# Head outputs of an attention layer turned by VectorE in 32x32 squares, a gap in the V products around it, and four more heads' maxima beside the experts

## What is computed

```python
xn = _layernorm(x)
# attention, per batch and head (64 in all)
a1 = softmax(q1 @ k1.T * scale) @ v          # v: 1024 x 16
a2 = softmax(q2 @ k2.T * scale) @ v
o = a1 - lam * a2
o = _rms_norm(o, sub_norm_w) * (1 - LAMBDA_INIT)
attn = o.reshape(B, N, 256) @ w_proj.T + b_proj
# experts: each token goes to two of 8; 512 rows an expert and slot range
h = gelu(disp @ w_gate)                      # 1024 wide
eo = h @ w_down
out = x + attn + g1 * eo[f1] + g2 * eo[f2]
```

## Time and profile before

| | us |
|---|---|
| median of 3 runs (1751.41 to 1754.59) | 1751.65 |
| the profiled execution | 1751.97 |
| its span, first to last instruction | 1750.1 |

### The profile page before, as it was taken

How to read it: one execution, slowest core, us unless ns; L and a number is a source line. 1 busy time by engine, 2 the same in 40 slices (tenths; PEclk the granted TensorE clock), 3 DMA queues, 4 the chain that set the end, 5 groups by cost and what they waited for, 6 DMA issues and landing times.

```text
span 1750.1 us, 78852 instructions
## 1 busy us (share of the span) xinstructions
PE 1660.8 (95%) x34242; PEld 917.0 (52%) x34243; DVE 1477.7 (84%) x2482; ACT 1349.4 (77%) x2637; POOL 718.5 (41%) x1201
## 2 busy tenths in 40 slices
PE   6998999999999899999999999999999999999998
PEld 5556777777777444444444444444444444444437
DVE  7878778777777899999899999999999989998925
ACT  4464353444534699999999999999999999999994
POOL 0126566655553033324333343334733433533344
PEclk9989999999999999999999999999999999999999
DMA  8653332132311412222222222222222222222103
GB/s 263 216 194 116 115 111 90 63 106 93 104 58 31 132 54 62 62 60 60 62 59 59 61 62 60 62 59 58 60 61 60 59 62 59 58 60 60 55 22 104
DMA packets 120859, 142.37 MB, mean 81 GB/s; under 512 B 25152, under 2 KB 83136, under 8 KB 120512
## 3 DMA queue, kind: packets, MB, share of 16 engines
q1 hardware_dynamic: 114368, 120.54, 22.6%
q0 software_dynamic: 6144, 16.79, 3.4%
HBM read 102.92 MB, written 34.34 MB: 78 GB/s over the span
## 4 chain that ended last, share of the span: by engine, by line
PE 67%; ACT 22%; DVE 5%; issue 4%; DMA 1%; POOL 1%; SPq 0%; ACTq 0%; DVEq 0%
ACT arena_t L950 19%; PE banks L1433 18%; PE banks L1448 17%; PE banks L1486 10%; PE banks L1464 7%; PE banks L1466 3%; PE banks L1397 3%; ACT o_raw L933 2%; PE banks L1533 2%; PE banks L1412 2%; PE banks L1300 2%; DVE row_half L1168 1%; PE banks L1569 1%; DVE rest L1048 1%; DVE row_half L1161 1%
## 5 line engine op out<-in xcount | busy, mean ns | idle before, releaser
L950 ACT ACTIVATE arena_t<-banks 128x512 f32<-128x512 f32 x2048 | 1037.7, 658 | 64.7 <-PE banks L1433 62.1
L1168 DVE TENSOR_REDUCE row_half<-banks 128x1 f32<-128x512 f32 x1600 | 989.8, 680 | 90.3 <-PE banks L1412 88.0
L1433 PE MATMUL banks<-arena_q 50*32 50x512 bf16 x8192 | 733.7, 382 | 15.0 <-ACT arena_t L950 10.2
L1448 PE MATMUL banks<-arena_t,v_ring 64*17 64x256 f32 x16384 | 702.3, 377 | 40.7 <-ACT o_raw L933 35.6
L1412 PE MATMUL banks<-qk_ring 48*32 48x512 bf16 x6400 | 614.2, 383 | 4.5 <-issue 3.1
L1433 PEld LDWEIGHTS banks<-arena_q 50*32 50x32 bf16 x8192 | 215.2, 89 | 467.5 <-ACT arena_t L950 350.4
L1448 PEld LDWEIGHTS banks<-arena_t,v_ring 64*17 64x17 f32 x16384 | 281.1, 93 | 124.9 <-ACT o_raw L933 54.1
L1161 DVE TENSOR_REDUCE row_half<-banks 128x2 f32<-128x1024 f32 x224 | 260.6, 1219 | 39.7 <-PE banks L1397 39.7
L915 ACT ACTIVATE arena_t<-banks 128x512 f32<-128x512 f32 x128 | 76.5, 597 | 236.1 <-PE banks L1486 228.4
L1486 PE MATMUL banks<-rows_parts,w_parts 128*128 128x512 f32 x768 | 192.9, 400 | 2.5 <-DVE rows_parts L1107 2.5
L676 POOL TENSOR_TENSOR inv_sum<-inv_sum,half_factor 128x16 f32<-128x16 f32 x64 | 13.9, 218 | 438.2 <-DVE inv_sum L1240 438.2
(11 more groups left out here) (144 smaller groups left out, 1328.3 us busy)
## 6 DMA issues: line engine op xcount, KB each, us to landing
v_ring<-v_heads SPq DMA_DIRECT2D x128, 68.0 KB, 2.7
expert_rows<-arena_r SPq DMA_DIRECT2D x16, 512.0 KB, 3.1
q_stack<-arena_q SPq DMA_DIRECT2D x8, 768.0 KB, 3.5
k_stack<-arena_q SPq DMA_DIRECT2D x8, 768.0 KB, 4.3
qk_ring<-q_stack SPq DMA_DIRECT2D x128, 48.0 KB
qk_ring<-k_stack SPq DMA_DIRECT2D x128, 48.0 KB
arena_q<-q_stack SPq DMA_DIRECT2D x128, 48.0 KB
arena_q<-k_stack SPq DMA_DIRECT2D x128, 48.0 KB
```

Source lines behind the costliest of these rows:

```text
L950: nc.scalar.activation(probs[:, kg % PSLOTS, qh, :], banks[:, ST_BANKS[ring_place(i) % 3], :], ACT.Exp).then_inc(exp_done, 1)
L1168: nc.vector.tensor_reduce(row_half[:, g % 2, h, u:u + 1], banks[:, half_bank(n), :], AX.X, ALU.max, negate=True).then_inc(half_done, 1)
L1433: mm = pe.matmul(banks[column:column + QUAD, ST_BANKS[place % 3], :], score_qk[g % SCORE_SLOTS][rows, 1, KEYS * kg + QUAD * c:KEYS * kg + ...
L1448: mm = pe.matmul(banks[QUAD * c:QUAD * c + VP, OT_BANK + s, 0:CH // 2], v_ring[rows, g % SLOTS, kg % 2, kg // 2, :], probs[rows, kg % PSLO ...
```

## The change

The output of a head is now turned by VectorE itself: one transpose instruction on 128x512 values, straight from the two banks, square by square of 32x32 (`o_turn`), in step 5 of the next head, and inverted in step 7. So that squares come out as whole token tiles, the columns of q are put in another order, in TensorE's products for q (`q_tokens`: runs of 32 tokens instead of 512). ScalarE's two copies and TensorE's four transposes are gone. The V products of a head stand at steps 9 to 37 (`pv_step`), so that between step 5, with the last of head g-1, and step 9, with the first of head g, there is none. The maxima of 18 heads instead of 14 are made beside the experts, with 18 pairs a chunk instead of 14, in groups of three after f = 0, 2, 4 and 6 and two groups of three between the down products. In attention the steps 1, 5, 6, 12, 16, 21, 25 and 30 have no maxima, so 24 of 32 have. All eight low parts of a chunk are made by GpSimd.

```diff
--- before.py
+++ after.py
-LAG = 4
-TURN_AT = 16
-O_COPY_AT = 5
-INVERT_AT = 24
+PV_FIRST, PV_LAST = 9, 37
+TURN_AT = 5
+INVERT_AT = 7
 MAX_SLOTS = 3
 SCORE_SLOTS = 3
-EARLY_HEADS = 14
+EARLY_HEADS = 18
...
-HALVES = 26
+NO_MAXIMUM_AT = (1, 5, 6, 12, 16, 21, 25, 30)
+HALVES = STEPS - len(NO_MAXIMUM_AT)
...
-BETWEEN = 14
-POOL_LOWS = 6
+BETWEEN = 18
+INTERLEAVED = 6
...
+        def pv_step(kg):
+
+            return PV_FIRST + kg * (PV_LAST - PV_FIRST) // (KG - 1)
...
# the sync engine, start of attention
-                if g == 0:
-                    load_for_max(EARLY_HEADS + MAX_SLOTS - 1)
+                for h in range(EARLY_HEADS, EARLY_HEADS + MAX_SLOTS):
+                    if g == 0 and max_load_chunk(h) >= 2 * E:
+                        load_for_max(h)
...
# GpSimd, a chunk of the experts
-                for f in range(2, POOL_LOWS):
+                for f in range(2, FC):
                     hidden_low(n, f)
...
# ScalarE, attention
-            def copy_o(g):
-
-                act.wait_ge(pv_done, KG * (g + 1))
-                nc.scalar.copy(o_raw[:].rearrange("p (s n) -> p s n", s=2),
-                               banks[:, OT_BANK:OT_BANK + 2, 0:CH // 2]).then_inc(o_copied, 1)
-
-            def take_o(g):
-
-                act.wait_ge(o_turned, g + 1)
-                from_first(act, scaled_ready, g)
-                nc.scalar.copy(o_turned_sb[:], banks[:, TURN_BANK, :].rearrange("p (c q w) -> p c q w", c=4, q=4)[:, :, :, 0:VP]).then_inc(o_taken, 1)
...
-                    if i == TURN_AT and g > 0:
-                        take_o(g - 1)
...
-                    if i == O_COPY_AT and g > 0:
-                        copy_o(g - 1)
...
# VectorE, a chunk of the experts
-                for j in range(6, 9):
+                for j in range(6, 12):
                     smax(first + j)
-                for f in range(POOL_LOWS, FC):
-                    dve.wait_ge(hidden_high, FC * n + f + 1)
-                    nc.vector.tensor_tensor(hidden_parts[:, LO, f, :], hidden[:, LO, f, :], hidden_parts[:, HI, f, :].bitcast(F32),
-                                            ALU.subtract).then_inc(last_hidden_ready, 1)
...
# VectorE, attention
+            def o_turn(g):
+
+                dve.wait_ge(pv_done, KG * (g + 1))
+                from_first(dve, scaled_ready, g)
+                nc.vector.transpose(o_turned_sb[:].rearrange("p s t w -> p s (t w)"), o_columns()).then_inc(o_turned, 1)
...
                     n = half_at(g, i)
                     if n is not None:
                         half_max(n)
+                    if i == TURN_AT and g > 0:
+                        o_turn(g - 1)
                     if i == INVERT_AT and g > 0:
                         o_invert(g - 1)
...
# TensorE, products for q and k
+            def q_tokens(b, c, half):
+
+                return xn_t[:, c, b * N:(b + 1) * N].rearrange("p (t q i) -> p q t i", t=TB, q=P // QUAD)[:, 2 * half:2 * half + 2]
...
-                                       xn_t[:, c, b * N + half * CH:b * N + (half + 1) * CH],
+                                       qk_tokens(b, c, half) if m >= 2 else q_tokens(b, c, half),
...
# TensorE, attention
                 if kg == 0:
-                    pe.wait_ge(o_copied, g + 1)
+                    from_first(pe, o_turned, g)
...
# TensorE, a chunk of the experts
-                    if f == 5:
+                    if f == 4:
                         for j in range(6, 9):
                             expert_smax(n, j)
+                    if f == 6:
+                        for j in range(9, 12):
+                            expert_smax(n, j)
...
-                pe.wait_ge(smax_done, BETWEEN * n + 9)
-                for f in range(POOL_LOWS):
+                pe.wait_ge(smax_done, BETWEEN * n + 12)
+                for f in range(INTERLEAVED):
                     down_tile(n, f, 0)
                     down_tile(n, f, 1)
-                for t in range(2):
-                    for f in range(POOL_LOWS, FC):
-                        down_tile(n, f, t)
-                for j in range(9, 12):
+                for f in range(INTERLEAVED, FC):
+                    down_tile(n, f, 0)
+                for j in range(12, 15):
                     expert_smax(n, j)
+                for f in range(INTERLEAVED, FC):
+                    down_tile(n, f, 1)
                 for f in range(FC):
                     down_tile(n, f, 2)
-                for j in range(12, 14):
+                for j in range(15, 18):
                     expert_smax(n, j)
...
# TensorE, attention
-            def turn_o(g):
-                pe.wait_ge(o_copied, g + 2)
-                for c in range(4):
-                    mm = pe.transpose(banks[:, TURN_BANK, c * P:(c + 1) * P], o_raw[:, c * P:(c + 1) * P], ident[:])
-                mm.then_inc(o_turned, 1)
...
-            def pv_before(g, kg):
-
-                if kg >= LAG:
-                    pv(g, kg - LAG)
-                elif g > 0:
-                    pv(g - 1, kg - LAG + KG)
+            def pv_before(g, i):
+
+                for kg in range(KG):
+                    if g > 0 and pv_step(kg) == STEPS + i:
+                        pv(g - 1, kg)
+                for kg in range(KG):
+                    if pv_step(kg) == i:
+                        pv(g, kg)
```

More of the change, by code:

```diff
@@ L336, in build_program @@
         ROOT_STEPS = 13
-        TURN_LAST_AT = 2
         OUT_TILES = 2
@@ L398, in rows_bank @@
             return ROWS_BANK if n > 0 else FIRST_ROWS_BANK
-        late_heads = range(EARLY_HEADS - 1, G)
+        late_heads = range(next(h for h in range(G) if join_chunk(h) >= 2 * E), G)
         def from_first(eng, s, value):
@@ L421, in half_of, with st_bank, o_columns @@
             return EARLY_HEADS + g, j // 2, j % 2
-        def ring_place(i):
-            return i if i < TURN_AT else i + 1
-        def score_before(place):
-            return place if place < TURN_AT else place - 1
+        def st_bank(step):
+            return ST_BANKS[step % len(ST_BANKS)]
+        def o_columns():
+            return banks[:, OT_BANK:OT_BANK + 2, 0:CH // 2]
         def ot_bank(t):
@@ L565, in expert_step @@
                     load_for_max(n + 1)
-                for h in range(MAX_SLOTS, EARLY_HEADS + MAX_SLOTS - 1):
+                for h in range(MAX_SLOTS, EARLY_HEADS + MAX_SLOTS):
                     if max_load_chunk(h) == n:
@@ L581, in expert_step @@
                     load_down(e + 2, e % 2)
-                for h in range(EARLY_HEADS - 1):
+                for h in range(late_heads.start):
                     if join_chunk(h) == n:
```

114 lines of the change are left out of this document (48 added, 66 removed).

## The result

The changed kernel takes 1760.12 us (the median of 5 runs), the kernel before 1751.65. Four of the five lie between 1759.92 and 1760.20; the fifth, at 2231.50 us, ran in a slower state of the core, and runs of that kind are left out of every ratio here. The ratio is 1.0045, 95% interval 1.003 to 1.0061: 8 us slower, where 32 us faster was forecast; the range ended at 1743. The profiled execution took 1760.05 us.

A forecast was written before the change was run, and what follows sets the result against it. SP, nearly full before, was to become attention's bound once copies and transposes were gone. 1751.97 less 62.2 for attention plus 30 for the experts gave 1719.8, as a median 1719.5 us; range 1690 to 1743.

The forecast's parts named there:

- experts: Expert chunks: four more score pairs and a new wait cost 1.9 us a chunk, 30 us in 16 (16 to 42).
- SP to head 60: Attention: SP issues block 58's last DMA 1007.6 us after the first exponential, so head 60 begins at 1011.3.
- heads 60 to 62: End of attention: no maxima are loaded behind head 60, compute leads again, 3 x 16.0 us.
- SP's 980 us for blocks 1 to 58: Attention: SP's issues take 1018 us less 38 for four heads' loads and stores, 980 (957 to 1002).
- It is nobody's bound only because compute is no faster: Attention before the change: SP nearly full at 17.15 us a block, against 17.8 us a head for compute.
- The predicted wait: Expert chunks: down products wait for the maxima of the group of f = 6, 0.9 us a chunk.
- q's order: TensorE's products for q: runs of 32 values taken as 0 us; rival: slower by 29 us, 1748.5, chance 0.06.
- Compute at 16.0 us a head: Attention: ScalarE's floor 15.7 us a head without copies, compute taken as 16.0, with SP slower as the bound.
- SP does hold up: Attention, against the rival that SP holds nobody up and compute sets the pace: 1672 us, chance 0.13.
- the turn doesn't sit on VectorE: Attention, against the rival that a 2.7 us turn makes VectorE hold heads at 18.1 us: 1802 us, chance 0.08.
- the experts cost 40.6, not 60: Experts, against the rival that late VectorE also holds the next chunk: 60 us instead of 30, 1749, chance 0.07.
- the likeliest case: Whole kernel: the forecast of 1719.5 us with SP as attention's bound, own range 1703 to 1736, chance 0.66.

The follow-up runs named there:

- e1: Changed kernel with GpSimd's split of a late head's maxima moved ahead of the root refinement: 1753.2 us, 1.0026 of the kernel before.
- e2: Changed kernel with the loads of v issued by GpSimd instead of SP: 1743.5 us, 0.9966 of the kernel before.
- e3: Changed kernel with the edits of e1 and e2 together: 1721.3 us, 0.9847 of the kernel before.
- e5: Kernel before the change with the loads of v issued by GpSimd instead of SP: 1707.6 us, ratio 0.9777.
- e13: e8 with the edits of e2 and e7, and all but the first four gathers left out: 1726.9 us, 0.9872 of the kernel before.
- e8: Kernel before, old turn kept, with 18 heads' maxima beside the experts and 24 maxima in 32 steps of attention: 1749.1 us, ratio 1.0005.
- e7: e3 with another bank order for an expert chunk's fourth group, down products waiting for its second tile: 1668.2 us, 0.9543 of the kernel before.
- e10: e3 with all but the first four of GpSimd's 64 gathers left out: 1672.0 us, 0.9565 of the kernel before.
- e12: e7 with the down products waiting for the fourth group's third tile again: 1719.6 us, 0.9834 of the kernel before.

## Why the prediction was wrong, step by step

The sum missed the profiled execution by 40.2 us. In its own terms: experts 10.6, SP to head 60 22.6, heads 60 to 62 7.0.

- **The term that was mis-sized most: SP's 980 us for blocks 1 to 58, measured 999.1** (bound 1002). The mechanism was right (e1, e2, e3), and so was the base: the stretch before with its 1680 issues has gaps over 0.15 us of 19.1 us in all, which leaves 1020.6 us occupied (I took 1018). The four heads' 64 issues went off and the gaps shrank to 4.8 us, but the 1616 issues left took 994.3 us, not 980 to 983: an issue for v 0.71 us in the mean instead of 0.66, one of a store 0.52 instead of 0.49, the loads of scores and maxima as before (all four are means over the stretch's rows). I had let durations stand while the queue filled up; why these two kinds grow wasn't tested. A full queue alone isn't it for the stores: in e5, where SP has 53 us of gaps, one takes 0.53 us. With it go a block 1 that began 1.2 us later than reckoned (28.8 us behind the first exponential) and a head 60 that began at 1651.9 us, 5.9 and not 3.7 behind block 58's last issue.
- **The pace of compute that the turn was set against wasn't understood.** "It is nobody's bound only because compute is no faster" stands as far as the trace goes: before the change TensorE waits for no landing. But by all that the runs show, the 17.8 us a head held 0.7 to 0.8 us of interruptions behind gathers, which I put down to the copies and the waits behind them: with hardly any the old turn takes 16.9 to 17.0 (e13, e8, e5). So where the gathers don't interrupt, the old turn is about as fast as SP's 17.2 us a block after the change, and e8, with the old turn, is at least as fast as the changed kernel. The Trainium skill ("Perfetto Trace Analysis", What "DMA-bound" means) names a sequencer whose track is solid with DMA slices as one of the ways to be bound by DMA; the changed kernel agrees (994.3 of 999.1 us occupied, and TensorE waits for landings), while the kernel before shows that nearly solid isn't enough (1020.6 of 1039.7 us, and no such wait). The other rule, in "DMA: Bandwidth & Descriptors" (Issuing engines are not separate DMA queues), that starting DMAs on several engines saves only a time that is usually small, does not hold for the changed kernel: there e2 moved 2 issues a head and saved 14 us, and beside e1's edit the same move saved 32 (e3 against e1).
- **The experts: 40.6 us for 30.** An ordinary chunk takes 29.97 us, 2.27 more instead of 1.9. The predicted wait is there, 0.66 us at 359.12. e7, without it, has chunks of 28.95 us: so the wait and the start behind it cost 1.0 us (0.9 said), and the four pairs more with their group 1.25 (1.0 said). In chunk 8 VectorE waited 3.07 us for a store to land (384.74) that SP had issued behind the next expert's weights, and chunk 1 and the end of the last lost some 2 and 1 more. The bound of 42 held, and e7 shows that the wait was avoidable.
- **Heads 60 to 62: 55.0 us for 48.0.** `INVERT_AT` went from 24 to 7, and the rule that places GpSimd's splits compares with it. Heads 45 and 63, which join at step 11, slid behind an inversion and so behind the root refinement, the scaling and the gathers. Head 63's split kept VectorE 16.83 us (row 1691.48), and there SP hid nothing. I had followed the change on TensorE, VectorE and SP, not on GpSimd. Head 45's 10.65 us SP did hide (e1).
- **Right:** the turn takes 0.71 us (0.68 said) and TensorE hardly waits for it; SP's timeline has no gap to speak of; the end is 2 us shorter. q's order costs nothing:

```profile
L1347 PE MATMUL banks<-arena_t,w_qk 128*128 128x512 f32 x128 | 57.7, 610 | 0.0
```

- **Compute at 16.0 us a head** was hidden here; freed of SP it was 16.6, or 15.8 to 15.9 with few or no gathers that interrupt (e3; e10, e7). That 16.0 lies close to the latter is luck: gathers don't occur in its sum.
- Of the rivals, none came in: SP does hold up, the turn doesn't sit on VectorE, q's order is free, and the experts cost 40.6, not 60. The other side came from the likeliest case itself: both its terms went to the ends of their bounds that cost time (999 of 1002, 40.6 of 42), which I had added as independent, and a stall that I had not seen came on top.

## What to carry to other kernels

Where a queue's issues stand next to each other for a whole stretch, its gaps say how much a faster compute can win at most: here 19 of 1039.7 us. Whether it is the bound already, its fullness doesn't say; waits for landings do. And an experiment that moves issues to another engine moves that engine's other work in time. Compare the traces for what else changed (here the gathers that interrupt TensorE, 22 against 1) before a gain is put down to the queue. When a constant that rules place other work by is moved, look at what slides on every engine, also on the one with slack.

## What was not expected of the hardware

- An indirect gather of 128 rows issued by GpSimd (1.03 to 1.09 us) can hold TensorE up by 0.4 to 0.9 us, about 1 us behind its issue, with no semaphore between them (e3 against e10: 49 us over 60 gathers, 0.8 us each). The same program of attention ran almost without these interruptions where it started 13 us earlier (e7 against e12). They are in the kernel before as well (22 of 64). Which coincidence makes the difference is open.
- GpSimd issues a plain load of v in 0.64 us (median of 128 in e2), no longer than SP's 0.6 to 0.7, where it was busy 48% of attention.
